# Group norm moved one slot earlier with its residual additions split over three scans, the sigmoid's exponentials kept in PSUM, and A_log loaded from ScalarE's queue

## What is computed

```python
# layer 0: the taps of an image
pooled = x.mean(axis=(2, 3)); h = relu(batchnorm(pooled @ fc_w.T))
ch_att = sigmoid(h @ ch_w.T + ch_b)
sp_att = sigmoid(h @ sp_w.T + sp_b)            # nine values
ke_att = softmax(h @ ke_w.T + ke_b)            # four values
agg_w = sum_k(ke_att * sp_att * od_weight)
# layer 1: scan, group norm, silu, residual
A = -exp(A_log)
h = exp(dt * A) * h + dt * B * x;  y = sum_n(h * C) + x * D
x1 = (y * silu(z)) @ W_out
out = silu(group_norm(x1)) + x_in
```

## Time and profile before

| what | value |
|---|---|
| median of 3 runs | 14398.5 us (14397.29 to 14399.63) |
| the profiled execution | 14398.59 us |
| its span, first to last instruction | 14396.8 us |
| mean granted TensorE clock | 0.851 of full speed |
| busy share: POOL, DVE, PE, ACT | 96%, 95%, 77%, 71% |

### The profile page before, as it was taken

How to read it: one execution, slowest core, us unless ns; L and a number is a source line. 1 busy time by engine, 2 the same in 40 slices (tenths; PEclk the granted TensorE clock), 3 DMA queues, 4 the chain that set the end, 5 groups by cost and what they waited for, 6 DMA issues and landing times.

```text
span 14396.8 us, 149878 instructions
## 1 busy us (share of the span) xinstructions
PE 11107.7 (77%) x32512; PEld 3277.9 (23%) x32512; DVE 13717.4 (95%) x11828; ACT 10283.7 (71%) x17320; POOL 13786.2 (96%) x3076
## 2 busy tenths in 40 slices
PE   6778777777777777778777777777787777777777
PEld 2222222222222222222222222222222222222221
DVE  6999999999999999999999999999999999999999
ACT  5777777777777777777777777777777777777776
POOL 6999999999999999999999999999999999999999
PEclk8888888888888888888888888888888888888887
DMA  5555555555655555555556555655555555656554
GB/s 122 139 137 139 139 144 140 134 141 137 148 135 139 136 141 141 141 141 134 142 140 144 133 141 135 147 137 139 141 135 143 139 142 133 143 135 148 136 138 114
DMA packets 1068196, 1991.53 MB, mean 138 GB/s; under 512 B 123649, under 2 KB 124730, under 8 KB 1067066
## 3 DMA queue, kind: packets, MB, share of 16 engines
q1 hardware_dynamic: 1067066, 1979.43, 57.1%
HBM read 1626.62 MB, written 352.32 MB: 137 GB/s over the span
## 4 chain that ended last, share of the span: by engine, by line
POOL 62%; issue 36%; DVE 1%; POOLq 0%; ACT 0%; PE 0%; SPq 0%; DMA 0%; DVEq 0%; ACTq 0%
POOL hq L933 45%; POOL dbx L925 17%; DVE hq L823 0%; POOLq L932 0%; SPq L196 0%; DVE dbx L810 0%; POOLq L924 0%; ACT pp L604 0%; DVE o L848 0%; PE pp L361 0%; PE pp L325 0%; SPq L190 0%; DMA dtx_d<-sp 0%; PE pp L362 0%; ACT ps_a L585 0%
## 5 line engine op out<-in xcount | busy, mean ns | idle before, releaser
L933 POOL TENSOR_TENSOR hq<-hq,c_rep 128x2048 f32<-128x2048 f32 x2048 | 9246.4, 4538 | 471.6 <-ACT carry L591 471.4
L823 DVE TENSOR_TENSOR_SCAN hq<-ps_a,carry,dbx 128x512 f32<-128x512 f32 x7168 | 8655.1, 1264 | 271.0 <-ACT carry L591 97.4
L585 ACT ACTIVATE ps_a<-dt_rep,A_neg 128x512 f32<-128x512 f32 x8192 | 5569.7, 686 | 3582.7 <-DVE hq L823 3542.3
L925 POOL TENSOR_TENSOR dbx<-dtx_rep,b_rep 128x2048 f32<-128x2048 f32 x1024 | 4637.4, 4529 | 117.8 <-DMA dtx_rep<-dtx_d 117.8
L417 PE MATMUL ps_acc<-hq,dsum 128*32 128x512 f32 x16384 | 2408.3, 663 | 628.4 <-POOL hq L933 628.4
L810 DVE TENSOR_TENSOR dbx<-dtx_rep,ps_b 128x2048 f32<-128x2048 f32 x1024 | 2315.6, 2261 | 17.1 <-DMA dtx_rep<-dtx_d 17.1
L325 PE MATMUL pp<-xin,diag 128*128 128x504 f32 (+3 forms) x4608 | 2213.5, 608 | 6.0 <-ACT diag L617 6.0
L405 PE MATMUL ps_b<-dbl,bsel 41*128 41x512 f32 x2048 | 1296.5, 716 | 400.5 <-issue 215.0
L361 PE MATMUL pp<-x,W_taps 128*128 128x512 f32 x768 | 677.4, 980 | 947.8 <-DVE x L784 665.6
L823 DVE TENSOR_TENSOR_SCAN hq<-ps_a,dbx 128x512 f32<-128x512 f32 x1024 | 1188.3, 1206 | 48.8 <-ACT ps_a L585 30.0
L325 PEld LDWEIGHTS pp<-xin,diag 128*128 128x128 f32 x4608 | 793.1, 189 | 1398.1 <-issue 1398.1
(11 more groups left out here) (117 smaller groups left out, 10164.2 us busy)
## 6 DMA issues: line engine op xcount, KB each, us to landing
dt_rep<-dt_d SPq DMA_DIRECT2D x2048, 256.0 KB, 5.7
dtx_rep<-dtx_d SPq DMA_DIRECT2D x2048, 256.0 KB, 4.9
c_rep<-bc_d SPq DMA_DIRECT2D x1024, 256.0 KB, 5.4
b_rep<-bc_d SPq DMA_DIRECT2D x1024, 128.0 KB, 2.9
dt_d<-dt SPq DMA_DIRECT2D x256, 512.0 KB, 6.0
dtx_d<-sp SPq DMA_DIRECT2D x256, 512.0 KB, 2.8
out<-o SPq DMA_DIRECT2D x128, 512.0 KB, 3.9
xin<-in_x SPq DMA_DIRECT2D x192, 320.0 KB, 8.7
```

The source lines that it names most:

```text
L585: A(ps_a[:, i % RA, :], dt_rep[:, q // NQ, g, :], ACT.Exp, scale=A_neg[:, q // NQ, q % NQ, g:g + 1]).then_inc(exp_done, 1)
L823: v.tensor_tensor_scan(hq[:, q % HQ, g, :], ps_a[:, i % RA, :], dbx[:, slot(q), g, :], carry[:, q, g:g + 1] if c % CH else 0.0, ALU.mult, ...
L925: g.tensor_tensor(dbx[:, slot(q), :, :], dtx_rep[:, d, :, :], b_rep[:, c % 2, q % NQ // 2, :].unsqueeze(1).to_broadcast([P, DG, T]), ALU.m ...
L933: g.tensor_tensor(quad, quad, c_rep[:, c % 2, q % NQ, :].unsqueeze(1).to_broadcast([P, DG, T]), ALU.mult).then_inc(cmul_done, 1)
```

## The change

In group norm, the moments move from slot 26 to 25, the scale from 28 to 27 and the SiLUs from the end of slot 30 to the start of slot 29, ahead of that slot's decay; the inverse root of the norm over channels (`rstd`), which uses the same PSUM bank, is moved ahead of them. The eight additions, in one block behind scan 31 before, stand behind scans 29, 30 and 31 as 3, 3 and 2. The nine exponentials are written to PSUM (`pp[:, 1, 48:57]`) instead of `att`. The 32 DMAs of `A_log` go to ACT's queue with a semaphore of their own, waited for only ahead of the first decay, and ACT does the exponential and the negation of A there. The first chunk's `dt*x` is spread ahead of `dt`. `keep_first`, a copy at an image's second chunk, waits for one addition fewer.

```diff
-GN_STATS, GN_SUM, GN_MOM, GN_RSTD, GN_SCALE, GN_SILU, GN_ADD = 24, 25, 26, 27, 28, 30, 31
+GN_STATS, GN_SUM, GN_MOM, GN_RSTD, GN_SCALE, GN_SILU = 24, 25, 25, 27, 27, 29
+GN_ADD = {29: (0, 1, 2), 30: (3, 4, 5), 31: (6, 7)}
...
-            for j in range(NJ):
-                for e in range(4):
-                    for d in range(DI):
-                        sp_e.dma_start(A_neg[DW * j + DSUB * e:DW * j + DSUB * e + DSUB, d, :, :],
-                                       al[j, e, d]).then_inc(w_loaded, 16)
...
             for d in range(DI):
+                spread_dtx(0, 0, d)
                 spread_dt(0, 0, d)
-            for d in range(DI):
-                spread_dtx(0, 0, d)
...
+            for j in range(NJ):
+                for e in range(4):
+                    for d in range(DI):
+                        act.dma_start(A_neg[DW * j + DSUB * e:DW * j + DSUB * e + DSUB, d, :, :],
+                                      al[j, e, d]).then_inc(a_loaded, 16)
             act.wait_ge(w_loaded, 16 * n_weights)
...
-            A(A_neg[:], A_neg[:], ACT.Exp).then_inc(setup_act, 1)
...
-                A(e9, s13[:, 0:9], ACT.Exp, scale=-1.0)
+                A(pp[:, 1, 48:57], s13[:, 0:9], ACT.Exp, scale=-1.0)
...
-                act.wait_ge(x1_done, b * CH + 3)
+                act.wait_ge(x1_done, b * CH + 2)
...
+                    if c == CH and u == GN_SILU:
+                        rstd(b, c + 2)
+                        group_silu(b)
                     if u + RA < NT:
...
-                        if u == ACT_RSTD:
+                        if u == ACT_RSTD and c != CH:
                             rstd(b, c + 2)
...
-                    if c == CH and u == GN_SILU:
-                        group_silu(b)
...
             rstd(0, 1)
+            act.wait_ge(a_loaded, 16 * DI * NJ * 4)
+            A(A_neg[:], A_neg[:], ACT.Exp).then_inc(setup_act, 1)
+            act.wait_ge(setup_act, 3)
+            A(A_neg[:], A_neg[:], ACT.Copy, scale=-1.0).then_inc(setup_act, 1)
...
-                v.tensor_scalar(den9, e9, 1.0, chs, ALU.add, ALU.mult).then_inc(att_step, 1)
+                v.tensor_scalar(den9, pp[:, 1, 48:57], 1.0, chs, ALU.add, ALU.mult).then_inc(att_step, 1)
...
-                        if u == GN_ADD:
-                            for k in range(CH):
-                                add_residual(b, k)
+                        for k in GN_ADD.get(u, ()):
+                            add_residual(b, k)
```

More of the change, by code:

```diff
@@ L156, in x1_cols @@
             return (x1n if c < 2 else x1)[:, 1 - shift + c * T:1 - shift + (c + 1) * T]
-        s13, e9, den9 = att[:, 0:13], att[:, 13:22], att[:, 22:31]
+        s13, den9 = att[:, 0:13], att[:, 22:31]
         ke, ksum, kmx, ech, chs = att[:, 31:35], att[:, 35:36], att[:, 36:37], att[:, 37:38], att[:, 38:39]
@@ L174, in build_program @@
         x_loaded = [x_loaded_even, sem("x_loaded_odd")]
-        wait_taken, kept, att_step = sem("wait_taken"), sem("kept"), sem("att_step")
+        wait_taken, kept, att_step, a_loaded = sem("wait_taken"), sem("kept"), sem("att_step"), sem("a_loaded")
         dt_repd = [sem("dt_repd_0"), sem("dt_repd_1")]
@@ L178, in build_program @@
         bc_repd = [sem("bc_repd_even"), sem("bc_repd_odd")]
-        n_weights = len(names) + 1 + DI * DG * NJ
+        n_weights = len(names) + 1
         block = ctx.enter_context(nc.Block())
@@ L191, in _ @@
             sp_e.dma_start(Wz[:], a["W_in"][:, 2 * P:4 * P]).then_inc(w_loaded, 16)
-            al = a["A_log"].rearrange("(s m j) (h e g) -> j e h s m g", s=DSUB, m=NQ, j=NJ, h=DI, e=4, g=DG)
-            for j in range(NJ):
-                for e in range(4):
-                    for d in range(DI):
-                        sp_e.dma_start(A_neg[DW * j + DSUB * e:DW * j + DSUB * e + DSUB, d, :, :],
-                                       al[j, e, d]).then_inc(w_loaded, 16)
             def load_pool(b, c):
@@ L497, in _ @@
             A = nc.scalar.activation
+            al = a["A_log"].rearrange("(s m j) (h e g) -> j e h s m g", s=DSUB, m=NQ, j=NJ, h=DI, e=4, g=DG)
+            for j in range(NJ):
[3 more added lines that the diff above has]
+                                      al[j, e, d]).then_inc(a_loaded, 16)
             act.wait_ge(w_loaded, 16 * n_weights)
@@ L707, in _ @@
             rstd(0, 1)
+            act.wait_ge(a_loaded, 16 * DI * NJ * 4)
+            A(A_neg[:], A_neg[:], ACT.Exp).then_inc(setup_act, 1)
+            act.wait_ge(setup_act, 3)
+            A(A_neg[:], A_neg[:], ACT.Copy, scale=-1.0).then_inc(setup_act, 1)
+            act.wait_ge(setup_act, 4)
             for i in range(RA):
@@ L743, in _ @@
             v.tensor_scalar(nch_b[:], w["ch_b"][:], -1.0, None, ALU.mult)
-            dve.wait_ge(setup_act, 3)
-            v.tensor_scalar(A_neg[:], A_neg[:], -1.0, None, ALU.mult)
             for k in range(2):
```

## The result

| kernel | median us (range) | ratio to before, 95% interval |
|---|---|---|
| before | 14397.9 (14396.86 to 14399.63) | 1 |
| after | 14148.11 (14145.18 to 14149.68) | 0.9826 (0.9812 to 0.9841) |

What follows compares the result with a forecast made beforehand. POOL and DVE set the pace; only POOL's 471.4 us idle behind ACT's carry copy and the start can shrink. Taps 123 + group norm 68 + start 20 = 211 us, so 14398.5 - 211 = 14187.5 us, range 14135 to 14250.

Steps and rivals of the forecast that it cites:

- What bounds the kernel: Whole kernel: POOL and DVE set the pace; only POOL's 471.4 us idle behind ACT's carry and the start can shrink.
- Taps: Chunk 5: L764 holds until POOL goes idle; a PSUM source removes 3.97 us in each of 31 images, 123 us.
- first rival: Chunk 5: the hold moves to the reciprocal (L767), the 123 us are gone, 14310.5 us; chance 0.13.
- Group norm: Iteration's end: of POOL's 10 us idle 7.8 remain, 31 x 2.2 = 68 us saved; bounds 25 and 112 us.
- steps 1 to 4: Group norm's new order: last quad starts 600.65, scans and product end 605.1, SiLUs start near 605.15, additions end 613.85.
- Step 5: Iteration's end: the branch costs its 3.78 us as before; next scan at 617.6, 2.2 us sooner, carry at 617.5.
- frees no work: Group norm: spreading additions over scans 30 and 31 leaves the sequence as long; only the idle 3.59 us is filled.
- step 1: Group norm: the scale a slot earlier makes DVE wait for ACT's inverse root; last quad starts 1.4 us later.
- second rival: Iteration's end: hand-overs cost more than counted, carry as late as before, group norm gives nothing, 14255 us; chance 0.10.
- the slower one: Iteration's end: decays behind the SiLUs delay the next carry, for example by 8 us an image, 14504 us; chance 0.03.
- The start: Program start: ACT begins 14.3 us sooner and the new spreading order gives 5.6 us, 20 us together.
- two queues hold each other up: Program start, lower bound: if SP's and ACT's queues held each other up, ACT's sooner start would give 0.

Runs made afterwards that it cites:

- e7: After with one more nine-element SBUF-to-SBUF tensor_scalar on DVE in chunk 2 of each of 31 images; 14411.43 us.
- e5: Before with only group norm's edits (and keep_first's), but all eight additions in one block behind scan 31; 14307.7 us.
- e6: After with group norm's scale put back from slot 27 to slot 28; 14154.07 us.
- e9: After with the scale back at slot 28 and the finished image's four stores issued once DVE has done the next chunk's first scan; 14096.74 us.
- e2: Before with only group norm's edits, the additions in three parts and keep_first's shorter wait; 14301.35 us.
- e10: After with the 32 A_log loads on SP's queue again, behind everything else it issues at the start; 14145.64 us.
- e8: Before with eight more one-column memsets on DVE in its setup; 14413.54 us.
- e1: Before with only the nine exponentials written to PSUM; 14262.24 us.
- e3: Before with only the start changed: A_log loads on ACT's queue and dt*x spread first; 14361.9 us.

## Why the prediction was right, step by step

**What bounds the kernel.** Right: the gain is POOL's idle time and the start, to 1 us (table above), and each single part and e7 moved the time through POOL's waits. Of the 39 us that the forecast fell short, some 34 are group norm's. The sum has one slip: with the bounds that the prediction gives for group norm (25 to 112 us) and for the start (3 to 29 us together), the times run from about 14134 to 14248, not from 14123 to 14251. The result lies inside either.

**Taps.** Right. The step "a hold until POOL goes idle, gone with the source in PSUM" gave 123 us and measured 125.7. 31.1 us are left, 1.00 an image, as said. e7 shows the hold itself, and that a hold's length is not that of one product: in the taps it was, because POOL had only one left to run. The first rival (the reciprocal) is false: 0.20 us beside a running product. That agrees with the Trainium skill (Vector Engine (DVE) Microarchitecture Reference, section 5.1), whose list of operations with the two-port mode has no reciprocal.

**Group norm.** Right in mechanism, off in one term. In this image, counted from the end of POOL's product ahead of the last quad (599.13 before, 1012.41 after), steps 1 to 4 came out within 0.1 us: the last quad's start at +1.50, forecast 600.65 or +1.52; the end of the additions at +14.63, forecast 613.85 or +14.72. Step 5 failed: "the branch costs its 3.78 us as before". It measured 2.86, and the next scan came at +17.49 where +18.47 was forecast. That is the difference between 2.2 us an image and the measured 102.5 / 31 = 3.3. The same holds on ACT, whose 1.93 us of issue ahead of the carry were taken over too and measured 0.68: the carry came at +17.04, forecast 617.5 or +18.37. The 3.78 us were no price of a branch but three things: some 3.4 us that run from the last wait met, not from the last instruction; one or two additions in its shadow; and about 1 us behind the stores. The statement that the spread "frees no work" held in e5, where the block costs 6 us more than the three pieces. The reason that the prediction gave for the limit, 1.4 us given back in step 1, was right for the scans. Taking it back gained nothing while the stores were in flight (e6); with the stores gone and the scale at slot 28, e9 is 51 us below after. How these 51 divide between the two edits is open, as after with late stores alone was not run. The second rival (group norm gives nothing) and the slower one are false: e2 gains 97 us, and the carry came no later than the scan.

**The start.** Right in sum, 21.6 for 20 us. Its pieces were off by little: ACT's first activation at 25.48 (forecast 25.1) is 13.9 us sooner for 14.3, and the new order of spreading gave the other 7.7 us for 5.6, the first product at 105.87 (107.5). That two queues hold each other up was named as a bound. SP's issues were slowed, 0.67 us for 0.43, but ACT's were not: 23.36 us for the 32 loads that took SP 22.98 in the earlier trace rows. It cost nothing, since ACT's own issues ended after the weights had come; e10 prices these issues, standing in ACT's program, at 7.4 us of start.

**What stays open.** Which packet of instructions DVE waits for at the branch; where e8's 15 us arise; why chunk 5 keeps 31.1 us in after, less, 24.7, in e1, and more, 44.8, in e9; why e3's branch is shorter than before's with the stores in the same place; and whether the packet count is the cause of ACT's shorter stand or goes with it.

## What to carry to other kernels

An idle time behind a loop's last instruction isn't a constant: measure it from the last wait that was met, and look at what the DMA engines carry just then, since the next instructions come the same way. Bulk stores that nobody waits for were better issued behind the branch in both kernels tried, by 57 and 31 us. And a tiny VectorE operation from SBUF to SBUF can cost as much as GpSimd has in stock; look for one whose mean is microseconds, and give it an operand in PSUM.

## What the runs showed of the hardware

- The instruction stream shares the DMA engines with data. With 2 MB of stores in flight the first instruction packet behind the last SiLU started 2.99 us after it and DVE stood for 4.51 us at the branch (e6); with the stores issued later it was 1.16 and 1.94 us (e9), means of 30 images.
- A nine-element tensor_scalar from SBUF to SBUF held DVE for 10.65 us in the median, through three GpSimd products of 4.5 us, not only the one that ran; a reciprocal of the same shape took 0.20 us beside one, and so did the tensor_scalar with its source in PSUM (0.23 us).
- While ACT's queue issued the 32 small loads of `A_log`, SP's weight loads took 0.67 us an issue in place of 0.43; ACT's own took 0.73, and the same loads issued by SP alone 0.72.
- Eight memsets of a column in the setup cost 15 us in the loop, 0.1% of the time, by a way that the runs don't show; a difference of that size between two programs need not come from what they do.
